# Seven more filler products on TensorE in the first chunk of a recurrence, behind the leaf scores of levels one to three

## The reference

```python
dxa = x_last - x                        # difference to the token before
xm = x + dxa * miu_x
lora_h = tanh(xm @ A_lora)              # five mixing factors, rank 32 each
miu = lambda_ + einsum(lora_h, B_lora)
w_in, k_in, v_in, r_in, g_in = x + dxa * miu
k, v, r = k_in @ Wk.T, v_in @ Wv.T, r_in @ Wr.T
g = silu(g_in @ Wg.T)
w = td_miu + tanh(w_in @ td_A) @ td_B   # decay = exp(-exp(w))
# per head, for each token t:
#   y_t = r_t @ (S + u * k_t^T v_t);  S = diag(decay_t) S + k_t^T v_t
out = (groupnorm(y) * g) @ Wo.T
```

## Time and profile before

| | us |
|---|---|
| median of 3 runs | 690.58 |
| lowest, highest | 685.58, 691.32 |
| the profiled execution | 684.28 |
| its span, first to last instruction | 682.2 |
| step 0 in the trace | 27.2 to 44.2 |

### The profile page before, as it was taken

The page is one execution under the profiler, slowest core; times in us unless marked ns, Lnnn a source line. Parts: engine busy times, 40 slices in busy tenths (PEclk is TensorE's granted clock), DMA queues, the critical chain, the costliest instruction groups (busy, mean ns, idle before and its releaser), DMA issues.

```text
span 682.2 us, 26441 instructions
## 1 busy us (share of the span) xinstructions
PE 641.0 (94%) x10978; PEld 547.5 (80%) x10978; DVE 421.7 (62%) x1384; ACT 302.7 (44%) x1017; POOL 254.8 (37%) x387
## 2 busy tenths in 40 slices
PE   5899999999759989999999999999999999999995
PEld 4567777777649977888888888888887999989995
DVE  3777777777633326577777686868676554444442
ACT  1456666643025414545545554545454353333331
POOL 1455666556710031131525252524243432322325
PEclk9899999999969999999999999999999999999999
DMA  7899200000048210000000000000221667566462
GB/s 191 287 299 308 57 3 2 4 6 19 25 137 244 82 43 7 7 9 7 20 12 20 14 18 16 16 16 12 97 77 26 225 223 240 186 214 225 154 241 62
DMA packets 50486, 65.69 MB, mean 96 GB/s; under 512 B 5168, under 2 KB 40208, under 8 KB 47424
## 3 DMA queue, kind: packets, MB, share of 16 engines
q1 hardware_dynamic: 44992, 57.22, 26.8%
q0 software_dynamic: 2912, 6.03, 2.6%
q10 hardware_dynamic: 2464, 0.76, 0.5%
HBM read 49.45 MB, written 18.87 MB: 100 GB/s over the span
## 4 chain that ended last, share of the span: by engine, by line
PE 59%; DVE 2%; DMA 1%; ACT 1%; issue 0%; SPq 0%; DVEq 0%
PE bank L1924 7%; PE quad L1782 6%; PE quad L1906 6%; PE quad L1908 5%; PE bank L1807 4%; PE pair L1744 3%; PE bank L1830 3%; PE quad L1788 2%; PE pair L1746 2%; PE pair L1745 2%; PE bank L1840 2%; PE pair L1769 2%; PE bank L1843 2%; PE bank L1833 2%; PE bank L1926 1%; PE quad L1911 1%
## 5 line engine op out<-in xcount | busy, mean ns | idle before, releaser
L2183 DVE TENSOR_TENSOR h_masked<-quad,const 128x1536 f32<-128x1536 f32 (+2 forms) x66 | 112.6, 1706 | 59.9 <-PE quad L1788 54.1
L2021 ACT ACTIVATE f_sa<-quad 128x256 f32<-128x256 f32 (+1 forms) x115 | 40.3, 352 | 91.6 <-PE quad L1908 75.8
L2202 DVE TENSOR_TENSOR f_hid<-f_sa,quad 128x256 f32<-128x256 f32 (+1 forms) x115 | 43.1, 380 | 53.6 <-ACT f_sa L2021 53.5
L2403 POOL DMA_INDIRECT moe_slots<-g_pay,g_slot x28 | 28.9, 1034 | 77.2 <-PE bank L1852 68.7
L1924 PE MATMUL bank<-wall,f_hid 128*128 128x128 f32 x390 | 50.7, 277 | 1.1 <-DVE f_hid L2205 0.9
L1924 PEld LDWEIGHTS bank<-wall,f_hid 128*128 128x128 f32 x390 | 47.8, 192 | 3.6 <-DVE f_hid L2205 2.8
L1906 PE MATMUL quad<-f_xT,wall 128*128 128x256 f32 (+1 forms) x190 | 50.0, 345 | 0.5 <-DVE f_hid L2202 0.5
L1908 PE MATMUL quad<-f_xT,wall 128*128 128x256 f32 (+1 forms) x190 | 49.2, 341 | 0.0
L1998 ACT ACTIVATE h_gT<-bank 128x128 f32<-128x128 f32 x64 | 17.8, 278 | 66.2 <-PE bank L1833 66.2
L1782 PE MATMUL quad<-h_qk 32*128 32x128 f32 x1024 | 46.5, 296 | 0.3 <-DVE h_masked L2183 0.3
L1782 PEld LDWEIGHTS quad<-h_qk 32*128 32x128 f32 x1024 | 34.3, 185 | 9.5 <-issue 7.0
(11 more groups left out here) (414 smaller groups left out, 1791.2 us busy)
## 6 DMA issues: line engine op xcount, KB each, us to landing
wall<-moe_w SPq DMA_DIRECT2D x23, 1088.0 KB, 5.1
moe_slots<-blank SPq DMA_DIRECT2D x2, 2112.0 KB, 24.4
wall<-in_experts_dram SPq DMA_DIRECT2D x1, 4120.0 KB, 21.8
e_w<-in_experts_dram SPq DMA_DIRECT2D x15, 257.5 KB, 3.3
moe_slots<-blank SPq DMA_DIRECT2D x1, 1984.0 KB, 9.7
moe_slots<-e_yg SPq DMA_DIRECT2D x7, 256.0 KB, 3.7
f_xg<-moe_slots SPq DMA_DIRECT2D x12, 132.0 KB, 4.1
moe_w<-in_moe_w_dram SPq DMA_DIRECT2D x1, 1408.0 KB, 7.2
```

The costliest lines, as they stand in the source:

```text
L2021: act.activation(sa[g % 3][:, 0:s], up_bank(n, f)[:, 0:s], ACT.Silu).then_inc(f_sa, 1)
L2183: dve.tensor_tensor(masked[k % 4][:, :, a * P:z * P], quad[:, :, a * P:z * P], cst("causal")[:, None, a * P:z * P].to_broadcast([P, HPG, ( ...
L2202: dve.tensor_tensor(hid[n % 2][:, f, 0:s], sa[g % 3][:, 0:s], up_bank(n, f)[:, T1:T1 + s], ALU.mult)\
L2403: pool.indirect_dma_start(out=t["moe1_slots"], out_offset=bass.IndirectOffsetOnAxis(ap=slot[:, b * 2 + k:b * 2 + k + 1], axis=0), in_=pay[ ...
```

## The change

In `step` of TensorE, a new branch behind the leaf scores puts three fillers behind those of level 1 and two each behind those of levels 2 and 3, in steps without a tail, which is step 0 alone. No wait and no other instruction is added, and no other engine's program changes. The two new lines move the line numbers behind them by two.

```diff
                     if tail and m == 1:
                         keep_busy(2)
                         transpose_heads(i - 1, 1 - q)
+                    elif not tail and m < 4:
+                        keep_busy(3 if m == 1 else 2)
                     if prepare and m == 2:
                         lora(i + 1)
                     elif m == 2:
```

## The result

The changed kernel takes 684.64 us (681.14 to 687.54, 20 runs), the kernel before 688.10 beside it (685.53 to 691.83, 20 runs): a ratio of 0.9933, 95% interval 0.9913 to 0.9952. By that ratio it is 4.6 us faster (0.0067 x 688.1), where +0.2 us was forecast. On another chip the same kernel gave 683.77 against 688.53, 0.9920 (0.9894 to 0.9945).

What follows compares the result with a forecast made beforehand. Step 0's end was taken to be set by when the mix (L1066) is done; fillers' delay, mostly swallowed by the 0.86 us pause, left +0.2 us, put on the 690.58 median: 690.8 us, range 684.3 to 692.6.

Steps and rivals of the forecast that it cites:

- rival (b): Fillers buy clock in step 0: where an execution loses full clock there, they give back at most 3.2 us; chance 0.15.
- The sum at full clock: Step 0 at 2.4 GHz: fillers delay the mix, the pause swallows 1.0 us, L507 and step 0 end +0.2 us late.
- the pause: 0.86 us TensorE standstill amid step 0's four L1063 mix products, read as a late code block; forecast to move into leaf scores.
- the bound +0.0: Lower bound of the +0.2 us term in step 0: the code block is there in time, then VectorE's 35.48 decides.
- lora comes later for nothing: In step 0 lora runs 0.60 us late, using up 0.64 us of VectorE idle time before L507, so it costs nothing.
- Rival (a): The pause belongs to step 0's mix, not code, and recurs behind the fillers: 1.3 us later, 691.9 us; chance 0.15.
- Rival (c): 28 instructions shift every later code-block boundary, some 85: within 1 us either way, 689.8 to 691.8; chance 0.15.

Runs made afterwards that it cites:

- front fillers: Five fillers added in the wait ahead of step 0: ratio 1.0014 on the kernel before, 0.9964 on the changed kernel; with copies held to step 5, 0.9935 and 0.9984.
- the split: Changed kernel plus five fillers ahead of step 0, rearranging copies early, only `wall` and the clearing of `moe1_slots` held until step 5: 684.74 us, 0.9949 to the kernel before.
- light fillers: Changed kernel with its seven fillers at 2 columns in place of 256, same instructions and places: 1.0002, repeated 0.9990, to the kernel before.
- quiet form: `wall` and `moe1_slots` clearing held until step 5, second mixture's weight layout ready from the host: 684.16 us on the kernel before, 684.53 on the changed one.

## Why the prediction was wrong

**The step that failed** is "The change doesn't touch what makes that spread, so I put the sum on the median". It touches just that: the change took the time at the low clock from 33 to 37 us down to 22.5, and the executions over 689 us from 40 in 148 to none in 32. I had one execution with the full clock in step 0 and took it as the kernel; 148 others, by their clock (0.974 on the median, 0.983 in that one), were at the low clock for some 12 us more (2 x 0.009 x 684), and took 3.3 us more on the median (687.6 to 684.28). The spread of 5.7 us over three runs, beside a profiled execution 6.3 us under their median, should have been priced and not set aside. Of the 6.2 us between 690.8 and 684.64, 2.5 are the base alone: the median of three runs was 690.58, that of twenty 688.10. That 684.64 lies inside the stated range is luck: its lower end took in a third of rival (b), whose price in step 0 turned out not to be the gain (and 685.58 less a third of 3.2 is 684.5, not 684.3).

**The sum at full clock** was as forecast. Two traces with the copies held to step 5 (without and with the front fillers) have step 0 with the seven fillers at full clock and no front filler in its way: it takes 17.06 us in both, 17.14 before, -0.1 for +0.2. With the rearranging copies where they were, the split's 17.19 is +0.05. The difference is the pause: the block came in time, or nearly (in the split the fourth leaf scores took 0.60 us instead of 0.38), the case of the bound +0.0. The seven fillers cost 3.5 us there and not 3.2, and that lora comes later for nothing holds: L507 (L508 in those kernels) starts 8.23 us into the step, 8.29 before. No run shows the changed kernel itself at full clock in step 0 with all copies in place.

**The pause is the code's**, as read: it moves by six records with 12 instructions and by ten with 20, it ends 1.3 to 1.7 us after a code packet, and the same program has 1.87 us of it with busy queues and none with free ones. Rival (a) falls with that. The Trainium skill's sentence that a crossing is mostly hidden (Runtime: NRT & Kernel Launch, Instruction fetch mechanics) holds where the queues are nearly idle (at most 0.50 us), and doesn't with busy ones: 0.86, 2.64 and 3.18 us stand against it.

**Rival (b)** had 0.15 and the right sign. Its first half is shown: the low stretch behind the front is 17.06 us without the fillers and 6.83 with them, 13.65 or more and 6.83 or less over twelve traces. The Trainium skill's rule that activity releases the throttle (TensorE: Matmul & The Clock Gate, Part 1), which I had found without support in step 0, agrees with that. Its price (at most 3.2 us for a fall in step 0) agrees with the 3.0 measured. But the fillers don't give it back: they run at the low clock themselves, and keep lora waiting; 0.6 us remain, and without traffic nothing measurable.

**Rival (c)** was undersized: "within 1 us either way" is 7 us in the trace in which the pause comes with a fall, since I had priced the pause and not the clock behind it.

**Where the 4.6 us come from.** Taking the traffic out of steps 0 to 5, without the fillers, gives 0.9956 and 0.9937; the fillers with traffic give 0.9933 and 0.9920; both together 0.9977 and 0.9949, no more than either. Executions over 689 us vanish in both. So the gain needs the traffic, and it is in the main the same loss that both take away: that is shown by the times. That this loss is late code blocks and the falls behind them is argued, from the traces that have them; traffic could cost in another way too, which no run here tells apart. Nor do the worst executions make up the gain: without the 35 at 0.971 or below the kernel before would average 687.0, 0.9 us less, and the changed one averages 684.2. No trace of the kernel before is of an execution above its median, so where the other 2.8 us go hasn't been seen. By which step the fillers' work would keep a block from being late, or from costing, is not shown either: the light fillers have the same code layout and don't do it, and with one or two traces for each kernel I can't say whether TensorE, fast again from 32 us on, reaches the block ends of steps 1 and 2 at better moments, or shows a late block less. It stays open.

## What to carry to other kernels

A profile is one execution: where a kernel's runs spread by more than the change is expected to bring, look at the granted clock of each run first, and ask of which of them the trace is. Long straight-line code on TensorE has to be brought in blocks while it runs, and full DMA queues make the blocks late: where a pause is marked issue, look whether the code queue's packet ends just before the restart. Whether bulk copies can be moved has to be tried: in steps 3 to 5 they cost 7 to 8 us, behind step 5 their absence from steps 0 to 5 gained about 3, and in three of four traces they then brought a pause of 1.9 to 3.2 us in the tail. A filler behind a fall is paid at the low clock. An ablation with the same instructions but few columns tells a filler's work from its place.

## What the runs showed of the hardware

With full queues a code packet can start some 7 us after the block end before it: in the trace with the 2.64 us pause, TensorE passed that end near 60.3, the packet started at 67.7, and TensorE worked again at 70.5. In the recurrence and its tail a fall of the clock went with each pause of 1.48, 1.87, 1.92, 1.95, 2.15, 2.55, 2.64, 2.80, 3.16 and 3.18 us, and with none of 1.00, 0.90, 0.88 or 0.86 us; the falls lasted 3.4 to 10.2 us. That is no rule for other places: near 248 us every trace has a pause of 1.85 to 2.92 us, and no code packet ends in the 2 us before it, with a fall in some (1.92, 1.95, 2.56) and none in others (1.87, 1.95, 2.65). In a stretch at the low clock TensorE seems busy for most of it (15.19 of 17.06 us), so that its busy share hides the loss. The time at the low clock and the time of the run go together within a kernel (0.43 us for each us, correlation 0.90, in 20 executions of the changed kernel; 0.39 and 0.88 in the quiet form of it). That isn't what less low time would bring: between the two quiet kernels 6.7 us less of it brought nothing.
